# Where the first expert layer's weights are split: during the softmax attention (24 pieces, ScalarE and GpSimd) or during the retention (48 pieces, ScalarE and VectorE)

## The reference, cut to what matters

```python
x = x + softmax_attention(layernorm(x))          # L0_attn
x = x + retention(layernorm(x), ctx, ctx)        # L0_xattn, 16 heads of 16
x = x + experts(layernorm(x), Wg, W1, W2, W3)    # L0_ffn: 8 experts, 2 chosen, hidden 512
x = x + lie_rotation(layernorm(x))               # L1_attn
x = x + one_key_attention(layernorm(x), ctx)     # L1_xattn
x = x + experts_and_shared(layernorm(x))         # L1_ffn
```

## Time and profile before

| | |
|---|---|
| median of 3 runs | 1789.09 us (1786.96 to 1796.44) |
| the profiled execution | 1801.88 us, span 1800.2 us |
| granted TensorE clock over the span | 0.797 |
| softmax attention | to 239.0 us |
| retention | 239.0 to 578.8 us |
| weight pieces loaded, stored | 12.6 MB, 12.6 MB |

### The profile page before, as it was taken

How to read it: one execution, slowest core, us unless ns; L and a number is a source line. 1 busy time by engine, 2 the same in 40 slices (tenths; PEclk the granted TensorE clock), 3 DMA queues, 4 the chain that set the end, 5 groups by cost and what they waited for, 6 DMA issues and landing times. The chain is left out here.

```text
span 1800.2 us, 33922 instructions
## 1 busy us (share of the span) xinstructions
PE 1308.9 (73%) x12427; PEld 1007.2 (56%) x12427; DVE 1085.2 (60%) x2003; ACT 768.1 (43%) x1302; POOL 740.7 (41%) x647
## 2 busy tenths in 40 slices
PE   3776737777874439999999538855788762299997
PEld 2555524666663428888888438622556542266665
DVE  4778744777764475555555492663788747644443
ACT  2455534566652513333333243231677761243443
POOL 1343336999983203444444232150677891000000
PEclk9877868888976559999999855556888865599999
DMA  4434376746630801222212260017633300000000
GB/s 176 131 120 130 113 175 127 120 95 124 101 48 16 361 9 54 62 63 62 60 61 61 101 232 1 2 33 120 137 69 61 61 2 0 1 13 19 16 23 24
DMA packets 96321, 143.49 MB, mean 80 GB/s; under 512 B 13108, under 2 KB 69558, under 8 KB 94136
## 3 DMA queue, kind: packets, MB, share of 16 engines
q1 hardware_dynamic: 87544, 116.95, 26.0%
q0 software_dynamic: 8640, 24.65, 4.4%
HBM read 85.56 MB, written 47.97 MB: 74 GB/s over the span
## 5 line engine op out<-in xcount | busy, mean ns | idle before, releaser
L2829 POOL TENSOR_TENSOR q_pl<-q_ex,q_ph 128x512 f16<-128x512 f32 x128 | 147.2, 1161 | 42.2 <-ACT q_ph L2790 41.5
L1776 POOL TENSOR_TENSOR r_siml<-r_sim,r_simh 128x512 f16<-128x512 f32 x128 | 146.0, 1162 | 15.3 <-ACT r_simh L1678 15.0
L1074 POOL DMA_INDIRECT expert_results<-mt_yout,m_deliver x78 | 77.4, 992 | 172.2 <-ACT mt_yout L1162 160.1
L2645 DVE TENSOR_REDUCE q_mx<-q_pS 128x4 f32<-128x512 f32 x128 | 86.6, 684 | 63.5 <-PE q_pS L2573 62.7
L1535 DVE TENSOR_TENSOR r_sim<-r_pS,r_causal 128x512 f32<-128x512 f32 x128 | 86.5, 681 | 54.2 <-PE r_pS L1449 50.4
L1107 PE MATMUL mt_pU<-mt_xh,m_w 128*128 128x256 f16 x624 | 116.2, 274 | 1.5 <-DVE mt_xl L1183 1.5
L1678 ACT ACTIVATE r_simh<-r_sim 128x512 f16<-128x512 f32 x128 | 80.0, 628 | 83.9 <-DVE r_sim L1535 79.7
L1107 PE MATMUL mt_pV<-mt_xh,m_w 128*128 128x256 f16 x624 | 115.4, 273 | 0.0
L1118 PE MATMUL mt_pY<-m_w,mt_hh 128*128 x624 | 106.4, 272 | 11.0 <-DVE mt_hl L1197 10.9
L3049 DVE TENSOR_TENSOR s_hc<-s_h,s_pC 128x512 f32<-128x512 f32 x64 | 44.0, 688 | 101.9 <-ACT s_h L3018 101.9
L1066 POOL DMA_INDIRECT mt_xin<-token_rows,m_fetch x78 | 76.0, 974 | 68.1 <-SPq L1058 44.6
(11 more groups left out here) (505 smaller groups left out, 4126.5 us busy)
## 6 DMA issues: line engine op xcount, KB each, us to landing
a_pf<-in_L_ffn_W SPq DMA_DIRECT2D x24, 512.0 KB, 4.0
m_w<-split_w SPq DMA_DIRECT2D x6, 2048.0 KB, 22.1
split_w<-a_ph SPq DMA_DIRECT2D x24, 256.0 KB, 2.0
split_w<-a_pl SPq DMA_DIRECT2D x24, 256.0 KB, 2.8
r_kstack<-k_bounce SPq DMA_DIRECT2D x48, 128.0 KB, 4.7
r_qstack<-q_bounce SPq DMA_DIRECT2D x48, 128.0 KB, 5.9
q_Q<-m_bounce SPq DMA_DIRECT2D x24, 256.0 KB, 6.1
X<-in_x SPq DMA_DIRECT2D x4, 1024.0 KB, 8.0
```

Of the source, the lines that this page charges most:

```text
L1074: pool.indirect_dma_start(results[:, :], bass.IndirectOffsetOnAxis(ap=deliver[:, at:at + 1], axis=0), yout[n % 2][:, a, :], None).then_inc ...
L1776: pool.tensor_tensor(siml[n % RING][:, :], sim[n % SIMS][:, :], simh[n % RING][:, :], ALU.subtract)\
L2645: dve.tensor_reduce(mx[:, at:at + UNIT], pS[n % 2][:, :, :], AX, ALU.max).then_inc(s["taken"], 1)
L2829: pool.tensor_tensor(pl[n % RING][:, :], ex[n % 3][:, :], ph[n % RING][:, :], ALU.subtract)\
```

## The change

The pieces leave the softmax attention, whose ACT and POOL lists become hardware loops as PE's and DVE's are. The retention gets them: 48 pieces of 512 columns, one every 4 steps, still two in flight, in the free first part of `ahead`. Piece n is loaded by SP at step -44+4n, rounded with its factor by one ACT instruction at -40+4n, its low part is taken by one DVE instruction one step later, and SP stores both halves at -38+4n. POOL has none of it.

```diff
@@ softmax_attention
-        WIDE, RING, PER = 1024, 2, 3
...
-                for n, (source, w, at) in enumerate(pieces):
-                    sp.wait_ge(piece_low, n + 1)
...
-                    act.activation(pf[n % RING][:, :], pf[n % RING][:, :], ACT.Copy, scale=256.0).then_inc(piece_scaled, 1)
-                    act.wait_ge(piece_scaled, n + 1)
-                    act.activation(ph[n % RING][:, :], pf[n % RING][:, :], ACT.Copy).then_inc(piece_high, 1)
...
-                for g in range(1, NG - 1):
+                with act.Fori(1, NG - 1) as g:
                     main(g, False, g + 1)
...
-                    pool.tensor_tensor(pl[n % RING][:, :], pf[n % RING][:, :], ph[n % RING][:, :], ALU.subtract)\
-                        .then_inc(piece_low, 1)
...
@@ retention
+        WIDE, PIECES_IN_FLIGHT, FIRST_PIECE, STEPS_PER_PIECE = 512, 2, -40, 4
...
+        def piece_due(t, lag):
+            n, rest = divmod(t - FIRST_PIECE - lag, STEPS_PER_PIECE)
+            return n if rest == 0 and 0 <= n < len(pieces) else None
...
+                def load_piece(n):
+                    source, w, at = pieces[n]
+                    if n >= PIECES_IN_FLIGHT:
+                        sp.wait_ge(piece_low, n - PIECES_IN_FLIGHT + 1)
+                    sp.dma_start(pf[n % PIECES_IN_FLIGHT][:, :], flat(source)[:, at:at + WIDE])\
+                      .then_inc(piece_in[n % PIECES_IN_FLIGHT], 16)
+
+                def store_piece(n):
+                    source, w, at = pieces[n]
+                    sp.wait_ge(piece_low, n + 1)
+                    for t, half in enumerate((ph, pl)):
+                        sp.dma_start(A["split_w"][w, t, :, at:at + WIDE], half[n % PIECES_IN_FLIGHT][:, :])\
+                          .then_inc(piece_out[n % PIECES_IN_FLIGHT], 16)
+
                 def step(t):
+                    n = piece_due(t, -4)
+                    if n is not None:
+                        load_piece(n)
+                    n = piece_due(t, 2)
+                    if n is not None:
+                        store_piece(n)
                     g = due(t, -46)
...
+                for i in range(PIECES_IN_FLIGHT):
+                    sp.wait_ge(piece_out[i], 32 * len(range(i, len(pieces), PIECES_IN_FLIGHT)))
...
+                    n = piece_due(t, 1)
+                    if n is not None:
+                        piece_lower(n)
+
+                def piece_lower(n):
+                    i = n % PIECES_IN_FLIGHT
+                    dve.wait_ge(piece_high, n + 1)
+                    dve.scalar_tensor_tensor(pl[i][:, :], pf[i][:, :], SCALE, ph[i][:, :], ALU.mult, ALU.subtract)\
+                       .then_inc(piece_low, 1)
...
+                    n = piece_due(t, 0)
+                    if n is not None:
+                        piece_upper(n)
+
+                def piece_upper(n):
+                    i = n % PIECES_IN_FLIGHT
+                    act.wait_ge(piece_in[i], 16 * (n // PIECES_IN_FLIGHT + 1))
+                    if n >= PIECES_IN_FLIGHT:
+                        act.wait_ge(piece_out[i], 32 * (n // PIECES_IN_FLIGHT))
+                    act.activation(ph[i][:, :], pf[i][:, :], ACT.Copy, scale=SCALE).then_inc(piece_high, 1)
```

More of the change, by code:

```diff
@@ L312, in eight @@
             return t[:, :, :].rearrange("p a (b t) -> p (a b) t", t=S)
-        WIDE, RING, PER = 1024, 2, 3
-        pieces = [(A[f"L0_ffn_{n}"], w, at) for w, n in enumerate(("W1", "W2", "W3"))
-                  for at in range(0, E * DC * HIDDEN, WIDE)]
-        pf = [c.sb(f"pf{i}", [P, WIDE]) for i in range(RING)]
-        ph, pl = ([c.sb(f"{n}{i}", [P, WIDE], f16) for i in range(RING)] for n in ("ph", "pl"))
-        piece_in, piece_out = ([c.sem(f"{n}{i}") for i in range(RING)] for n in ("piece_in", "piece_out"))
-        piece_scaled, piece_high, piece_low = (c.sem(n) for n in ("piece_scaled", "piece_high", "piece_low"))
         with nc.Block() as block:
@@ L329, in _ @@
                 ahead.load(sp, "retention")
-                def load_piece(n):
-                    source, w, at = pieces[n]
-                    sp.dma_start(pf[n % RING][:, :], flat(source)[:, at:at + WIDE]).then_inc(piece_in[n % RING], 16)
-                for n in range(RING):
-                    load_piece(n)
-                for n, (source, w, at) in enumerate(pieces):
-                    sp.wait_ge(piece_low, n + 1)
-                    for t, half in enumerate((ph, pl)):
-                        sp.dma_start(A["split_w"][w, t, :, at:at + WIDE], half[n % RING][:, :])\
-                          .then_inc(piece_out[n % RING], 16)
-                    if n + RING < len(pieces):
-                        load_piece(n + RING)
-                for i in range(RING):
-                    sp.wait_ge(piece_out[i], 32 * len(range(i, len(pieces), RING)))
             @block.tensor
@@ L485, in exps @@
                            .then_inc(kv[n, "exp"], 1)
-                def piece(n):
-                    act.wait_ge(piece_in[n % RING], 16 * (n // RING + 1))
-                    if n >= RING:
-                        act.wait_ge(piece_out[n % RING], 32 * (n // RING))
-                    act.activation(pf[n % RING][:, :], pf[n % RING][:, :], ACT.Copy, scale=256.0).then_inc(piece_scaled, 1)
-                    act.wait_ge(piece_scaled, n + 1)
-                    act.activation(ph[n % RING][:, :], pf[n % RING][:, :], ACT.Copy).then_inc(piece_high, 1)
                 def main(g, first, nxt):
-                    piece(PER * g)
                     act.wait_ge(s["nqmax_done"], g + 1)
@@ L502, in main @@
                     act.activation(vt[:, :, :], pC4, ACT.Copy).then_inc(s["vt_done"], 1)
-                    piece(PER * g + 1)
                     if nxt is not None:
@@ L507, in main @@
                     act.activation(aT[:, :, :].rearrange("p a b -> p (a b)"), pB[:, 0, :], ACT.Copy).then_inc(s["aT_done"], 1)
-                    piece(PER * g + 2)
                     if nxt is not None:
@@ L531, in main @@
                         .then_inc(s["vn_done"], 1)
-                    low(PER * g)
                     if nxt is not None:
                         fr.power_of_var(pool, nxt)
-                    low(PER * g + 1)
-                    low(PER * g + 2)
                 fr.power_of_var(pool, 0)
                 main(0, True, 1)
-                for g in range(1, NG - 1):
+                with pool.Fori(1, NG - 1) as g:
                     main(g, False, g + 1)
@@ L1311, in wait_low, with kept_apart @@
                 eng.wait_ge(s["low_pool"], n - lows_dve(n) + 1)
+        WIDE, PIECES_IN_FLIGHT, FIRST_PIECE, STEPS_PER_PIECE = 512, 2, -40, 4
+        pieces = [(A[f"L0_ffn_{n}"], w, at) for w, n in enumerate(("W1", "W2", "W3"))
+                  for at in range(0, E * DC * HIDDEN, WIDE)]
+        gate_w = ahead.held("moe_swiglu")[0].shape[1] if "moe_swiglu" in ahead.sources else 0
+        def kept_apart(i):
+            return ahead.area[:, gate_w + i * WIDE // 2:gate_w + (i + 1) * WIDE // 2]
+        pf = [ahead.area[:, gate_w + (2 + i) * WIDE:gate_w + (3 + i) * WIDE] for i in range(PIECES_IN_FLIGHT)]
+        ph, pl = ([kept_apart(2 * t + i).bitcast(f16) for i in range(PIECES_IN_FLIGHT)] for t in range(2))
+        piece_in, piece_out = ([c.sem(f"{n}{i}") for i in range(PIECES_IN_FLIGHT)] for n in ("piece_in", "piece_out"))
+        piece_high, piece_low = c.sem("piece_high"), c.sem("piece_low")
+        def piece_due(t, lag):
+            n, rest = divmod(t - FIRST_PIECE - lag, STEPS_PER_PIECE)
+            return n if rest == 0 and 0 <= n < len(pieces) else None
         with nc.Block() as block:
```

2 lines of the change are left out of this document (removed).

## The result

The changed kernel takes 1820.44 us in the median of 4 runs (1818.3 to 1824.68), the kernel before 1788.86 us in 4 runs of the same session (1786.96 to 1796.44). The ratio is 1.0167, 95% interval [1.0143, 1.0191]: 1.7% slower, some 30 us. The prediction was 1811.7 us.

The account below looks back on a forecast made before the run. Bounds: DVE's list in the attention, POOL in the retention's middle, latency in head and tail. -9.2 + 12.3 + 2 + 9 + 4 + 3 + 1.5 = +22.6 us took 1789.1 to 1811.7 us; range 1795 to 1834.

Parts of the forecast that it names:

- attention and its end: Softmax attention without the pieces: DVE's stalls behind POOL's subtraction and the wait for the last stores go, -9.2 us.
- head, turn_rows late: Retention's head: piece 0, in front of the first norm, lands late and starts the chain 12.3 us late.
- head, unit 0 late in all: Retention's head: first piece's 12.3 us plus 2 us for nine more pieces, +14.3 us.
- middle, POOL's busy time: Retention's middle: DVE's two-input piece instruction costs POOL 0.36 us a piece, 25 pieces, 9 us.
- middle, units waiting for DVE and ACT: Retention's middle: piece work on DVE and ACT delays mask and rounding, which POOL waits for, 4 us.
- last units: Retention's last units: eight pieces meet units that POOL does not pace alone, 3 us.
- tail: Retention's tail: gated_high waits behind piece 46's load and its ACT instruction, +1.5 us.
- Rival 4: Attention doesn't shorten because PE's product takes the stall's place: +6 us, 1818; chance inside the forecast's 0.66.
- Head, the rest: Retention's head: nine more pieces, mostly in gaps, two places a group on the chain, 2 us, bounds 0 and 5.
- Rival 1: Retention's middle and last units: the port costs POOL nothing, so +6.6 us, 1795.7; chance 0.14.
- rival 2: Retention's middle and last units: DVE becomes the bound, every piece costs 1.4 us, +52, 1841; chance 0.13.
- Rival 3: Head, retention's end and attention: TensorE's granted clock rises, making the kernel faster, 1776; chance 0.05.

Follow-up runs that it names:

- no_pool_low: The kernel before without POOL's subtraction of the pieces, the high half stored twice: 1780.66 us, ratio 0.9936 to before.
- before_again: The kernel before, unchanged, run and profiled once more: 1792.86 us.
- early_loads: The changed kernel with the loads of pieces 0 and 1 issued ahead of the zeros: 1813.53 us, ratio 1.0124 to before.
- dma_only: The changed kernel without ACT's and DVE's piece instructions; each load is followed by two same-size stores from a constant tile: 1791.84 us, ratio 1.0001 to before.
- dma_small_head: dma_only with the first twelve pieces' transfers cut to an eighth of their columns, the rest stored later; one execution, unit 0 at 75.6 us.
- one_input: The changed kernel with piece_lower replaced by a same-size DVE instruction reading one SBUF tile: 1809.27 us, ratio 1.0098 to before.

## Why the prediction was right, and where its sizes were off

Slower was right, and 1820.4 us lies in the range. The sum was 9 us short. Its steps, predicted against measured (profiles; for the attention the medians of nine and of two, for the middle of three and of five; one pair for the rest):

| step | predicted | measured |
|---|---|---|
| attention and its end | -9.2 | -10.4 |
| (head, turn_rows late, part of the next row) | (+12.3) | (+13.2) |
| head, unit 0 late in all | +14.3 | +18.6 |
| middle, POOL's busy time | +9 | +8.5 |
| middle, units waiting for DVE and ACT | +4 | +7.8 |
| last units | +3 | +4.8 |
| tail | +1.5 | +2.4 |
| sum | +22.6 | +31.7 |

The medians differ by 31.6 us.

**Attention.** The mechanism was right: no_pool_low shows that POOL's subtraction alone held DVE. The step took two small instructions, L418 and L84, for 6.3 us; their busy time fell by 4.8 and 1.6. A third one, L451, stalled in all eight groups, and the prediction left it out, because it has one input and I looked for two. Its 7 x (1079-158) ns = 6.4 us would have spoiled the sum, had it been added: they lie inside DVE's wait for ACT before L154, which grew by 6.5 us. Leaving it out was luck. The Trainium skill ("SBUF — State Buffer", section Who interferes with whom) also lists tensor_scalar among the operations that can take the shared pair; the trace agrees, with 1079 ns beside POOL's subtraction and 158 without it. So DVE lost 14.7 us of busy time, yet the updates of X end only 7.5 us earlier (medians 234.7 and 227.2). Rival 4 (PE takes the stall's place) isn't seen for the two that were counted. The end of the stage gave 3.8 us in the first pair and 2.0 against before_again (predicted 3.2).

**Head, first piece.** Right in kind and size. The pieces landed at 254.9 us, 28.3 behind the first transfer, where 266 against 239.04 was taken, 27.0.

**Head, the rest.** This is a step that failed in its reasoning. The prediction says that load_context(1) comes late "by about as much as the rest" and takes nothing for SP's order and the bytes in the head beyond a bound. early_loads shows that with turn_rows on time two thirds of the delay are still there (12.7 of 18.6 us), where the prediction had 2; dma_only that transfers with waits of SP alone make 11 us, and dma_small_head that about half of these stay with an eighth of the bytes. The two causes hide one another: taking away the first piece's wait gains 6 us, not 13. So the head's +14.3 came near 18.6 partly by luck.

**Middle.** POOL's price a piece was read from one instruction, L2125, as 0.36 us; it is 0.35. From a single row that is partly luck. (L2184 is stalled twice in that trace, for 4296 and 4269 ns, not once.) DVE's own instruction was put at 1.4 us, and the sign named was a median near that; the mean in the middle is 1.25, the median over all pieces 0.92. Rival 1 (the port costs nothing) is out: one_input takes POOL's busy time to that of before. By the Trainium skill's rule of the same section, the whole instruction (0.68 us a piece), it would by the prediction's estimate be 17 us in the middle; the trace has half of it. The mis-sized term is what reaches POOL through mask and sim_high: "I take 4 us", measured about 8. POOL's waits for ACT went from 6.6 us to 19.4; profiles of before's kind have up to 12.1, early_loads 13.5. DVE as the bound (rival 2) is out too: DVE is busy for 171 of 218 us.

**Tail.** The mechanism of gated_high is there. Behind the last low part it comes 17.1 us in place of 14.8, 2.4 later where 1.5 was predicted. ACT stood 5.27 us for a piece's load before it:

```profile
602.89 0.63 ACT L1746 ACTIVATE ahead<-ahead 128x512 f16<-128x512 f32 x1 [5.27 <-DMA ahead<-in_L_ffn_W]
603.43 1.01 ACT L1700 ACTIVATE r_gh<-r_pB 128x1024 f16<-128x1024 f32 x1
```

**Clock.** Rival 3 is out: 0.68 in the head and in the last units, 0.63 in the tail.

What stays open: how the 12 us between the changed kernel and one_input divide between POOL's 8.5 us and DVE's shorter instruction, since a profile's middle varies by some us between executions; how the changed kernel's head divides between SP's waits and the bytes; and what the bytes alone cost the middle (dma_only's 199.5 us lies inside the 196.6 to 202.3 of before's kind).

## What to carry to other kernels

Before work is moved away from a stage, ask which single instruction of it costs there: here one POOL subtraction that met three DVE instructions of 0.16 us, two of them on the path. Putting POOL behind a semaphore, into DVE's gap, gave what the move was to give, and its retention shows no price. A stall that a trace shows counts only if nothing behind it waits anyway: look at when the next large instruction begins. Work put into an in-order queue costs its waits, not only its time: price each wait by what stands behind it on that engine, SP's transfers included, and expect a second one under the first. A stage that is paced by POOL has no free DVE instructions with two SBUF inputs, and a chain of units has less slack than the idle time of its engines says.

## What the runs showed of the hardware

A DVE TENSOR_SCALAR of 128x4 float32, one SBUF tile in and one out, waits out a POOL instruction (1079 ns against 158), and so does a two-input TENSOR_TENSOR of 128x8 (841 against 167); TENSOR_REDUCE of 128x512 does not (676 ns, 687 at most, with POOL busy for 91% of the middle in one_input), nor a TENSOR_TENSOR with one input in PSUM (1.23 us). POOL's side of the meeting cost it 0.35 us a piece of 512 columns, less than DVE's 0.68. In the head of dma_small_head a load of 64 columns (32 KB) still took 2.4 us in the median to land. The same product (L396) took 1.99 us at a granted clock of 1.00 and 3.78 at 0.50, in different executions of the kernel before. The same kernel's experts' tiles took 349.0 us in one profile and 335.9 in another; why is open.
